# Graph network kernel, attention rounds: TensorE reads query rows before the softmax chain's small products and turns scanned states back one step later

## What is computed

```python
def _transformer_conv(x, src, dst, edge_attr, ...):
    q = x @ wq + bq; k = x @ wk + bk; v = x @ wv + bv
    e = edge_attr @ we
    ke = k[src] + e
    score = jnp.sum(q[dst] * ke, axis=-1) / jnp.sqrt(64)
    smax = jax.ops.segment_max(score, dst, num_segments=n_nodes)
    a = jnp.exp(score - smax[dst])
    alpha = a / jax.ops.segment_sum(a, dst, num_segments=n_nodes)[dst]
    msg = alpha[:, None] * (v[src] + e)
    return jax.ops.segment_sum(msg, dst, num_segments=n_nodes) + x @ ws + bs
h1 = relu(_transformer_conv(x, ...)); h2 = relu(_transformer_conv(h1, ...))
```

## Time and profile before

| what | value |
|---|---|
| median of 3 runs | 8052.2 us (8051.64 to 8053.5) |
| profiled execution | 8052.15 us, of which the span of its instructions is 8050.2 us |
| busy over the span | POOL 5546.3 us (69%), PE 4278.3 (53%), DVE 2503.7 (31%), ACT 2071.7 (26%) |
| mean granted TensorE clock | 0.84 of full speed; 1.00 in both attention rounds |
| the two attention rounds | first gathers at 1161.60 and 2382.24 us, last states stored from 2286.2 and 3506.4 us |

### The profile page before, as it was taken

One profiled execution on the slowest core, in us unless ns is written; L12 is line 12 of the kernel. 1 busy time (PEld: TensorE's weight loads), 2 busy tenths in 40 slices (PEclk: granted clock), 3 DMA queues, 4 the chain that ended last, 5 costly groups with the idle time before them and its releaser, 6 DMA issues.

```text
span 8050.2 us, 123362 instructions
## 1 busy us (share of the span) xinstructions
PE 4278.3 (53%) x24036; PEld 2775.3 (34%) x24036; DVE 2503.7 (31%) x4334; ACT 2071.7 (26%) x6406; POOL 5546.3 (69%) x5874
## 2 busy tenths in 40 slices
PE   3444435555555555566333326666646666466664
PEld 2333324444444444442222213333323333233332
DVE  5444435555535555531333331111111111111112
ACT  1111114444424444431111111111111111111111
POOL 6777757666637666633777757777767777577776
PEclk9999999999999999999999996565555656556565
DMA  5566647777736767622222224444444544344443
GB/s 144 150 150 150 150 102 151 150 151 151 152 87 151 152 152 151 149 61 93 60 59 59 59 60 109 111 112 112 101 96 112 112 111 111 86 112 111 111 111 87
DMA packets 2187581, 925.65 MB, mean 115 GB/s; under 512 B 1607262, under 2 KB 2070694, under 8 KB 2181094
## 3 DMA queue, kind: packets, MB, share of 16 engines
q1 hardware_dynamic: 1078982, 458.38, 23.1%
q10 hardware_dynamic: 921120, 272.38, 14.6%
q0 software_dynamic: 187392, 193.93, 13.3%
HBM read 657.22 MB, written 266.58 MB: 115 GB/s over the span
## 4 chain that ended last, share of the span: by engine, by line
PE 45%; issue 36%; POOL 9%; DVE 4%; DMA 4%; ACT 2%; ACTq 0%; DVEq 0%; POOLq 0%
POOL edges_a L906 8%; PE ps L1213 8%; PE ps L1205 7%; PE ps L1136 6%; PE ps L1132 6%; PE ps L1148 5%; PE ps L1197 4%; PE ps L1122 3%; DMA edges_a<-src_table,idx 3%; PE ps L584 2%; PE ps L1113 1%; PE ps L635 1%; PE ps L577 1%; POOL edges_a L913 1%; PE ps L1181 1%
## 5 line engine op out<-in xcount | busy, mean ns | idle before, releaser
L906 POOL DMA_INDIRECT edges_a<-src_table,idx x4040 | 3821.5, 946 | 1519.6 <-issue 1165.5
L913 POOL DMA_INDIRECT edges_a<-src_table,idx x1616 | 1524.6, 943 | 768.5 <-issue 448.8
L1341 DVE TENSOR_TENSOR_SCAN st<-pen,st,ps 128x512 f32<-128x512 f32 x300 | 383.9, 1280 | 2591.9 <-PE ps L1205 2591.7
L1132 PE MATMUL ps<-ident,edges_a 128*128 128x128 f32 x1212 | 563.5, 465 | 1173.1 <-issue 1024.6
L1213 PE MATMUL ps<-ident,st 64*128 64x64 f32 (+2 forms) x4444 | 926.2, 361 | 430.3 <-issue 395.1
L1122 PE MATMUL ps<-ident,edges_a 128*64 128x128 f32 x1616 | 419.1, 415 | 1255.1 <-DVE edges_a L1359 672.7
L1213 PEld LDWEIGHTS ps<-ident,st 64*128 64x128 f32 (+2 forms) x4444 | 704.9, 215 | 1043.9 <-issue 997.0
L1341 DVE TENSOR_TENSOR_SCAN st<-edges_a,st,ps 64x512 f32<-64x512 fp8e4 x402 | 511.2, 1272 | 874.9 <-issue 475.8
L1132 PEld LDWEIGHTS ps<-ident,edges_a 128*128 128x128 f32 x1212 | 219.3, 181 | 1428.8 <-issue 1266.4
L1040 ACT ACTIVATE edges_a<-ps,b 128x512 f32<-128x512 f32 x303 | 208.2, 687 | 1912.6 <-PE ps L1136 1912.6
L1122 PEld LDWEIGHTS ps<-ident,edges_a 128*64 128x64 f32 x1616 | 216.4, 158 | 1337.7 <-issue 1256.5
(11 more groups left out here) (189 smaller groups left out, 3531.6 us busy)
## 6 DMA issues: line engine op xcount, KB each, us to landing
states_sum<-hb ACTq DMA_DIRECT2D x1010, 128.0 KB
win_sb<-dst_table SPq DMA_DIRECT2D x1616, 72.8 KB
edges_a<-src_table,idx POOLq DMA_INDIRECT x5656
states_att<-hb ACTq DMA_DIRECT2D x404, 194.0 KB
win_sb<-dst_table ACTq DMA_DIRECT2D x1212, 48.0 KB
win_sb<-dst_table SPq DMA_DIRECT2D x1212, 48.0 KB
dst_b<-in_dst_row SPq DMA_DIRECT2D x50, 1024.0 KB, 5.7
sel<-onehots SPq DMA_DIRECT2D x303, 128.0 KB
```

Of the source, the lines that this page charges most:

```text
L906: pool.indirect_dma_start(rows[:, s, j * D:(j + 1) * D], None, srcs[q.r], bass.IndirectOffsetOnAxis(ap=idx[:, s, j:j + 1], axis=0))\
L913: pool.indirect_dma_start(xe_a[:, s, j * KA:j * KA + D], None, srcs[q.r], bass.IndirectOffsetOnAxis(ap=idx_a[:, s, j:j + 1], axis=0))\
L1132: nc.tensor.matmul(bank(TURNED, s)[:, at_j], rows[:, s, j * P:(j + 1) * P], ident[:, :], is_transpose=True, start=True, stop=False)
L1341: nc.vector.tensor_tensor_scan(st[0:w, s % V, :], d0, d1, init, op0, op1).then_inc(q.st_ready.sem, 1)
```

## The change

The jobs keep their work and their waits. PE's list gets a new order; `turn_run` is cut in two jobs, the second of which is `spread_kept`; `back` goes from lag LW + 1 = 6 to LW + 2 = 7; and ACT's `states_out` and `store_states` go one step later with it.

```diff
@@ -1063,7 +1063,7 @@
 
                 if k == ATT:
                     chunks(act, q.steps, (B + 2, kept), (B + 2, weights), (B + LW, weigh), (B + LW, decays), (0, indices_att),
-                           (B + LW + 2, states_out), (B + LW + 3, store_states), ring=UA)
+                           (B + LW + 3, states_out), (B + LW + 4, store_states), ring=UA)
                 elif k == MAX:
                     if q.r == 4:
                         for h in range(2):
@@ -1177,6 +1177,12 @@
                     wait(pe, (q.run_ready, 4 * g + 3), (q.ref_ready, g))
                     nc.tensor.matmul(run_t[0:m, :], run_in[:, 0:m], ident[0:1, 0:1], is_transpose=True,
                                      start=True, stop=True).then_inc(q.run_turned.sem, 1)
+
+                def spread_kept(c, s, n):
+
+                    if not group(c, s, n):
+                        return
+                    g, gs_, m = group(c, s, n)
                     wait(pe, (q.kept_ready, g + 1), (q.weight_out, g))
                     nc.tensor.matmul(kept_ps[:, 0:m], ones_row[:, :], kept_row[:, 0:m],
                                      start=True, stop=True).then_inc(q.kept_spread.sem, 1)
@@ -1216,8 +1222,8 @@
                     last.then_inc(q.back.sem, 1)
 
                 if k == ATT:
-                    chunks(pe, q.steps, (1, turn_scores), (2, turn_run), (2, turn_weights), (0, query), (1, turn_ends),
-                           (LW, turn_weighted), (LW + 1, back), ring=UA)
+                    chunks(pe, q.steps, (0, query), (2, turn_run), (1, turn_scores), (2, spread_kept), (2, turn_weights),
+                           (LW, turn_weighted), (LW + 2, back), (1, turn_ends), ring=UA)
                 elif k == MAX:
                     chunks(pe, q.steps, (0, turn_pair), (1, lift), (2, back))
                 else:
```

## The result

The changed kernel takes 7873.2 us (median of 4 runs, 7872.7 to 7874.4), the kernel before 8052.9 us beside it (8051.6 to 8054.8). The ratio is 0.9777, with a 95% interval of 0.9761 to 0.9792. The profiled execution took 7872.85 us for a span of 7871.0 us; against the profiled one of before that is 179.3 us less, where 190.0 were forecast.

What follows compares the result with a forecast made beforehand. The prediction took the order tying PE and DVE, not an engine, as the bound. With POOL then the limit, savings of 95.2 and 94.8 us in the two attention rounds took 8052.15 to 7862 us, eight-in-ten range 7855 to 7955.

Steps and rivals of the forecast that it cites:

- The closed ring: Attention rounds, PE and DVE: query, product, score, scan, back, query take 4.46 us per step; this order sets the group's 22.0 us.
- The steps of the group: Four steps after the change: step 2's product at 11.9 us, step 3's 15.1, next step 0's 18.3 after step 0's.
- what would show it: Signs in the profile: POOL share about 0.74, idle 0.30 us before L913, products 4.99 us apart and released by gather DMA.
- the forecast's own signs of being wrong: POOL still waiting over 0.3 us in each group, a clock under 1.00 in the two rounds, or products still waiting for L1148.
- `turn_ends` behind `back` at 0: PE's `turn_ends` after `turn_weighted` and `back`: costs 0 while PE is ahead, otherwise up to 2.0 us on the chain.
- POOL's limit of 19.97 us: Both attention rounds: POOL becomes the limit at 1.248 us per gather, 16 gathers per group; chance 75%.
- The landing of 1.9 us: Attention rounds: a product that waits for its gather starts 1.92 us after the gather's end.
- the two sums: Attention rounds from gather pace, landing and differences: last product at 2172.0 and 3392.6 us, saving 95.2 and 94.8 us.
- round 2's last product: Work behind it: same scans, turns and stores as before, change put at 0, with 1 us either way.
- the slack of the gate: POOL's gather into the slot L1022 frees: due at 13.4 us, can start at 9.4, so 4.0 us to spare.
- The rival of TensorE's clock: Attention rounds: PE falls to half clock from longer idling and becomes the limit, 8204 us; chance 5%.
- The partial rival: Part of POOL's wait stays, from late `turn_ends` or DMA: group 21.0 us, half the saving, 7957 us; chance 16%.

Runs made afterwards that it cites:

- The order alone: Changed kernel with `back`, hb and store at their old lags, so only PE's new list order is left: 8030.5 us, ratio 0.9972 to the kernel before.
- the later step alone: Kernel before, its list in the old order, with only `back` and ACT's hb and store one step later: 7878.5 us, ratio 0.9784.
- The three-gather kernel: Changed kernel with three gathers of four per step in the attention rounds, the fourth tile's source features zero: 7696.8 us, ratio 0.9556.
- the first set: Runs on one chip with the kernel before, unchanged, beside them; that kernel takes 8053.4 us (8051.1 to 8059.5, 17 runs).

## Why the prediction was right, and where its sizes were off

**The closed ring as the limit of before: right.** The order alone leaves the ring and brings 23 us, the later step alone opens it and brings 175. A quarter fewer gathers is worth 17 us before the change and 176 after it. A later `back` was the one edit that mattered; the three others cost nothing, as the parts said, and also bring next to nothing once the ring is open (7878.5 against 7873.2, from different sets, 5 us).

**The steps of the group: right in sum, wrong in one detail.** Step 2's product was forecast 11.9 us after step 0's and stands 11.76 after it (1911.64, 1923.40), the chain's end at 8.6 and stands at 8.80, PE's longest idle piece at some 3 us and is 3.27 (1913.78). The products are not evenly 4.99 us apart, as "what would show it" said: 5.29, 6.47, 4.79 and 4.17 in the group at step 44. PE still sets the second of them (4.06 us behind L1148, since step 2's query stands behind L1203, which needs the chain), and the two after it catch up with the gathers. A product that still waits for L1148 was one of the forecast's own signs of being wrong, and one of the four in each group does; its working had it so too (step 2's product at 11.9), and only the sign was put too strictly. The sum was made from POOL's pace alone, so this cost nothing.

**`turn_ends` behind `back` at 0: right here, for the reason given.** In the changed kernel `back` is over at 1910.51 and segments at about 1913.7, so L1168 never waits behind it. Put behind a `back` that waits for its scan, the same job costs the chain 1.6 us.

**POOL's limit of 19.97 us: right.** 20.04 was measured. The small rest is in the gathers: from the first to the last start of round 1 are 2171.62 - 1161.31 = 1010.3 us, forecast 1007.3, and in round 2 1009.2. That is 4.9 us of the 10.7 that were missing, and 3.1 of them are five odd gaps, which the forecast's own range for this case had allowed for: POOL is idle for 0.52 to 1.43 us in steps 28, 72, 116 and 160 of round 1 and 1.31 in step 28 of round 2, with nothing waited for that the profile shows.

**The landing of 1.9 us: the mis-sized term.** The step of the forecast says that "a product that waits for its gather starts 1.92 us after the gather's end", from one product at the start of a round. With POOL at its full pace the steps 40 to 180 of round 1 show 4.56 us in the mean for step 0's product and never under 3.69; at the end of round 1 it is 2177.04 - 2172.56 = 4.48 and in round 2 3306.70 - 3302.40 = 4.30. Against 1.9 + 0.2 that is 4.6 us in the two sums, and with the gathers 9.5 of the 10.7. Most of the rest is behind round 2's last product, which was put at 0: 4564.3 us to the end of the span, before 4562.8.

The term is one of the steady state and not of the change. In the trace of the kernel before, the semaphore events of a step 0's gathers end 4.2 us in the mean after the last gather (steps 40 to 180, the 34 groups of which at least nine in ten events are in the trace); its product came 7.70 us after them, behind L1148, so nothing waited and no row showed it. After the change they end 4.4 us after the last gather. Steps 1 and 2 have 1.5 to 2.6 us in both kernels, and step 3 goes from 2.1 to 4.7. What makes the landing so different between the steps of a group was not separated.

The same term sizes the slack of the gate, which was put at 4.0 us and is 1.44 in the group shown: step 148's gathers end at 1907.26, its product starts 4.38 later, L1022 ends 8.80 after that (1920.44), the restart takes 0.77, and the gather starts at 1922.65. Over the 36 groups of the steps 40 to 180 the gather starts 0.78 to 3.11 us after L1022's end, 1.91 in the mean, so the slack is 1.1 us in the mean and once nothing. The forecast was safe by this, not by 4 us. The three-gather kernel shows what happens with the margin gone: a landing of 5.8 us and a wait of 4.04.

A longer landing could have been looked for. The Trainium skill (DMA: Bandwidth & Descriptors, section "Latency and other measured facts") gives the latency of the memory as 0.2 us in the mean and 2 us under high load, and calls it the main part of a DMA's fixed cost. The direction agrees with this case, 1.9 us at the start of a round and 3.7 to 5.6 for step 0 at a DMA share of 0.76; the growth of 2.6 us in the mean is more than that figure holds.

**The rival of TensorE's clock: wrong, and from a misread column.** It took the 1.00 in the earlier trace rows as full speed, made PE's 12.9 us per group a figure of full clock, and stretched it for the slow one. The sum has a slip of its own: with 82% of the time at 1.2 GHz the work takes 12.9 / 0.59 = 21.9 us, not 23.5, so even by its premise PE would only have come level with the 22.0 of before. The rows of one matmul form in the relational round say otherwise, before and after:

```profile
L1122 PE MATMUL ps<-ident,edges_a 128*64 128x128 f32 x792 | 204.7, 414 | 672.8 <-DVE edges_a L1359 662.5 <-DMA edges_a<-src_table,idx 10.3
```

```profile
L1122 PE MATMUL ps<-ident,edges_a 128*64 128x128 f32 x792 | 204.6, 413 | 673.1 <-DVE edges_a L1365 662.5 <-DMA edges_a<-src_table,idx 10.7
```

414 and 413 ns, under a clock column of 1.00 in the earlier trace rows and of 0.50 after. The column shows 1.00 until the first record of the clock in a trace, at about 4854 us in the trace of before and 1209 us in the one of after. One trace shows it by itself: two stretches of the kernel before with three gathers, on either side of its first record (columns as in the earlier trace rows):

```profile
1300.00:2100.00 800.00, 468.26 (x3161) 387.63 (x3160) 413.28 (x744) 383.48 (x1347) 413.27 (x439) 1.00 0.69 145
2500.00:3200.00 700.00, 411.10 (x2767) 339.39 (x2767) 362.35 (x655) 335.92 (x1180) 359.38 (x382) 0.50 0.68 145
```

PE is busy for 0.585 and 0.587 of them with the same work, under 1.00 and under 0.50. The record says the same: 17 runs of the kernel before in the first set took 8051 to 8059 us, and their mean clock reads 0.61 eleven times, 0.68 to 0.69 three times and 0.84 three times. And every query of the two rounds of before takes 1.14 to 1.19 us. So the attention rounds of before ran at half clock (1.2 GHz) throughout, where the table ahead of the prediction has 1.00, the 12.9 us were those of the slow level, and the clock had no lower level to fall to. A clock under 1.00, the forecast's other sign of being wrong, so says nothing against it. What happened is the reverse. In the changed kernel the 12 matmuls of a query take 0.71 us at 1907.22, after PE had run since 1900.98 with a single wait, of 0.62 us, and 1.16 to 1.18 us after the pause of 3.27 us (1913.91, 1922.12). PE's work per group falls from 652.48 / 50.5 = 12.9 to 519.52 / 50.5 = 10.3 us. Is that where the gain is from? By the slow durations alone the forecast reached 18.3 us for PE, DVE and ACT, below POOL's 19.97, so the faster clock was not needed for it; no run here held the clock down to show it.

The rival had also set the relational round against the Trainium skill (TensorE: Matmul & The Clock Gate, section "HAM oscillation — how this bites in real kernels"), by whose rule bursts with long waits between them can fall back to the half clock. With the column read rightly, that round, with its waits of up to 4.28 us, sits at 0.50, and rule and trace agree.

**The partial rival** had a chance of 16% and 7957 us. Its two sources were both seen, the chain longer by `turn_ends` (in the order alone) and DMA late (4.56 us for 1.9), but neither fills the group on the first chip. The late DMA takes from a slack that was just large enough.

## What to carry to other kernels

Where two engines each wait a little for the other in every step, write down the ring that ties them and its length. An edit that shifts work inside such a ring only moves the wait to the next step, while a lag that takes one link out of it frees all of it, up to the next engine's pace. Then size each gate in front of that engine with durations from the steady state, for each step of a group by itself, and not from the start of a round, where transfers land fast. Where the row of the waiting instruction can't show a landing, because it waited for something later, the events of the transfer can. And before a column is taken for a state of the chip, check it by the duration of one fixed form of instruction in two stretches.

## What the runs showed of the hardware

The landing of a gather, from the end of the last DMA_INDIRECT of a step to the product that waits for it, is 1.9 us when a round starts and 4.56 in the mean for step 0 of a group at a DMA share of 0.76. By the semaphore events it differs between the steps of one group, 2.1 us in step 1 and 4.7 in step 3. TensorE ran the 12 matmuls of a query in 0.71 us and in 1.16 to 1.18 us within 7 us of each other, the longer after an idle piece of 3.27 us; the clock column has 1.00 over the first (1905.06 to 1910.50) and 0.50 over the second (1913.90 to 1916.00). And one kernel took 8053, 10264 and 10422 us on three chips, with gathers of 0.94 us and DVE scans of 1.27 us alike; the change gave a ratio of 0.978 and 0.980 on the two on which it ran.
